# Level clips left out, abs max and scales of two tiles at once, levels and outputs a tile later, in the FFN of a gated cross-attention block

## The reference, cut to what matters

```python
x = x + tanh(g_xattn) * attention(layernorm(x), ctx, ctx, ...)
x = x + tanh(g_ffn) * ffn(layernorm(x), w_gate, w_up, w_down)

def _act_quant(x):
    scale = 127.0 / clip(max(abs(x), axis=-1), 1e-05)
    return clip(round(x * scale), -128.0, 127.0) / scale
def _bitlinear(x, w):          # w is quantized to -1, 0, 1 times a scale
    return einsum('bsi,oi->bso', _act_quant(x), _weight_quant(w))
def ffn(x):
    gate = silu(_bitlinear(x, w_gate))
    up = _bitlinear(x, w_up)
    return _bitlinear(gate * up, w_down)
```

## Time and profile before

| what | us |
|---|---|
| median of 3 runs | 810.11 |
| lowest and highest | 806.78, 812.03 |
| span of the profiled execution, first to last instruction | 806.5 |
| first product of tile 0 (L1015) starts | 700.39 |
| last product, tile 27, starts | 793.34 |

### The profile page before, as it was taken

One profiled execution on the slowest core, in us unless ns is written; L12 is line 12 of the kernel. 1 busy time (PEld: TensorE's weight loads), 2 busy tenths in 40 slices (PEclk: granted clock), 3 DMA queues, 4 the chain that ended last, 5 costly groups with the idle time before them and its releaser, 6 DMA issues.

```text
span 806.5 us, 20948 instructions
## 1 busy us (share of the span) xinstructions
PE 708.8 (88%) x7117; PEld 475.3 (59%) x7127; DVE 720.1 (89%) x1479; ACT 691.7 (86%) x1482; POOL 520.3 (65%) x983
## 2 busy tenths in 40 slices
PE   7568889999999999999999999999998888777886
PEld 5234566666666666666666666666665555433444
DVE  5789899979899898989999999899999868798996
ACT  1578789898999999999999999999898997678884
POOL 4757556667777667676666676767663145376985
PEclk8666699999999999999999999999999999899999
DMA  9997847464667565767545666646563123156567
GB/s 206 202 259 179 176 123 148 106 114 129 153 119 145 123 141 123 147 115 151 127 129 141 126 130 133 128 128 138 114 124 73 45 72 97 52 124 165 137 164 176
DMA packets 148889, 108.50 MB, mean 135 GB/s; under 512 B 56992, under 2 KB 145184, under 8 KB 148768
## 3 DMA queue, kind: packets, MB, share of 16 engines
q1 hardware_dynamic: 143630, 101.98, 57.0%
q10 hardware_dynamic: 5152, 5.19, 2.6%
HBM read 49.54 MB, written 12.85 MB: 77 GB/s over the span
## 4 chain that ended last, share of the span: by engine, by line
PE 45%; DVE 22%; ACT 21%; issue 7%; DMA 2%; POOL 2%; SPq 1%; DVEq 0%; ACTq 0%; POOLq 0%
PE p_o L1327 9%; PE p_m L1405 9%; ACT ex L1179 7%; PE p_s L1310 7%; ACT pt L1169 6%; PE p_t L1348 5%; DVE kst L1015 4%; DVE hmax L1018 4%; PE p_m L1394 4%; DVE stats L890 3%; PE p_m L1386 3%; ACT L1169 2%; ACT L1206 2%; PE p_m L1378 2%; DVE nm L909 2%
## 5 line engine op out<-in xcount | busy, mean ns | idle before, releaser
L1179 ACT ACTIVATE ex<-p_s,nm 112x375 f32<-112x375 f32 x512 | 272.6, 606 | 10.1 <-DVE nm L909 8.9
L1169 ACT ACTIVATE pt<-p_t,ct 128x336 f32<-128x336 f32 x488 | 242.5, 563 | 32.4 <-PE p_t L1348 31.9
L890 DVE BATCH_NORM_STATS2 stats<-ex 112x6 f32<-112x375 f32 x512 | 253.2, 537 | 8.1 <-ACT ex L1179 6.6
L909 DVE TENSOR_REDUCE nm<-p_s 112x2 f32<-112x750 f32 x256 | 236.6, 925 | 2.0 <-PE p_s L1310 2.0
L1310 PE MATMUL p_s<-kst,qst 96*112 96x375 bf16 x512 | 135.8, 350 | 34.3 <-ACT ex L1179 24.8
L1348 PE MATMUL p_t<-qst,kst 99*128 99x112 bf16 x1464 | 115.3, 214 | 3.5 <-ACT pt L1169 2.7
L1348 PEld LDWEIGHTS p_t<-qst,kst 99*128 99x128 bf16 x1464 | 91.3, 98 | 42.9 <-issue 18.7
L1386 PE MATMUL p_m<-wv_sb,ctxt 128*128 128x256 f32 (+1 forms) x384 | 106.3, 400 | 4.0 <-DVE va L842 2.6
L1327 PE MATMUL p_o<-pt,va 128*32 128x112 f32 (+1 forms) x3072 | 102.0, 266 | 1.0 <-ACT ex L1179 0.5
L1405 PE MATMUL p_m<-ctxt,wk_sb 128*128 128x375 f32 x240 | 94.3, 517 | 1.3 <-DVE qf L858 0.7
L1327 PEld LDWEIGHTS p_o<-pt,va 128*32 128x32 f32 (+1 forms) x3072 | 70.8, 111 | 36.9 <-issue 30.7
(11 more groups left out here) (190 smaller groups left out, 1201.3 us busy)
## 6 DMA issues: line engine op xcount, KB each, us to landing
kst<-kp SPq DMA_DIRECT2D x378, 93.8 KB, 3.5
ctxt<-ctxt_dram SPq DMA_DIRECT2D x32, 375.0 KB, 4.2
qbounce<-qp SPq DMA_DIRECT2D x32, 168.0 KB, 2.7
qst<-qbounce SPq DMA_DIRECT2D x32, 168.0 KB, 3.6
qst<-qbounce SPq DMA_DIRECT2D x32, 112.0 KB, 3.4
xm<-x_dram SPq DMA_DIRECT2D x32, 112.0 KB, 2.4
x_dram<-x SPq DMA_DIRECT2D x32, 112.0 KB, 1.9
xt<-x_dram SPq DMA_DIRECT2D x28, 128.0 KB, 2.9
```

Source lines behind the costliest of these rows:

```text
L890: last = nc.vector.bn_stats(stats[:, nb % RING, 2 * pb + i], ex[0:SQ, 2 * (t % 2) + i, :])
L909: nc.vector.tensor_reduce(nm[:, n % RING, 2 * p:2 * p + 2], p_s[t % 2][0:SQ, :, 0:SK], axis=AX.X, op=ALU.max, negate=True).then_inc(s_max, 1)
L1169: nc.scalar.activation(pt[:, (2 * r + i) % 8], st_home(r, i)[:, 0:KC * SQ].rearrange("k (c q) -> k c q", c=KC), ACT.Exp, scale=ct[:, nr % ...
L1179: last = nc.scalar.activation(ex[0:SQ, 2 * ((t - 1) % 2) + i, :], p_s[(t - 1) % 2][0:SQ, i, 0:SK], ACT.Exp, bias=nm[:, ne % RING, h:h + 1])
```

## The change

- The clip of x levels (L712) and of hidden levels (L725, L1039) is left out. POOL and DVE convert the rounded values at once.
- The ring `hh` of products has 4 buffers in place of 2. DVE forms the products of two tiles and then takes the abs max, the scale and the reciprocal of both with one instruction each (`step_of`, `in_step`); the last two tiles, 26 and 27, stay apart.
- The output scale moves from ACT (L1243, each tile) to POOL, one for two tiles.
- ACT rounds tile s - 2 in step s, where it was s - 1. POOL, SP's transposing DMA, the down product and the outputs go a step later with it (`T_LAG` 2 to 3, `Y_LAG` 5 to 6). SP loads the residual rows of tile s - 2.

```diff
-HRING, XRING, T_LAG, Y_LAG, YRING = 4, 8, 2, 5, 4
+HRING, XRING, X_LAG, T_LAG, Y_LAG, YRING = 4, 8, 2, 3, 6, 4
+HHRING = 4
...
+        def step_of(n):
+
+            return n // GROUP if n < TILES - GROUP else n - (TILES - GROUP) // GROUP
+
+        def in_step(j):
+
+            return [n for n in range(TILES) if step_of(n) == j]
...
-                nc.gpsimd.tensor_scalar(fxn[:, i % 2], fxn[:, i % 2], ROUND + 127.0, ROUND - 128.0, ALU.min, ALU.max).then_inc(s_gk, 1)
-                pool.wait_ge(s_gk, count(1, i, 1))
...
             def tile(s):
-                n = s - 1
+                n = s - 2
                 if 0 <= n < TILES:
+                    j = step_of(n)
+                    if n == in_step(j)[0]:
+                        first, end = n, n + len(in_step(j))
+                        pool.wait_ge(s_hsc, count(1, j, 1))
+                        if j == 0:
+                            pool.wait_ge(s_tn, TN_TGD)
+                        nc.gpsimd.tensor_scalar(ysc[:, first:end], hsc[:, first:end], tgd[:, 0:1], 0.0, ALU.mult, ALU.add).then_inc(s_ysc, 1)
...
-                    nc.gpsimd.tensor_scalar(hr[n % HRING][:, half], hr[n % HRING][:, half], ROUND + 127.0, ROUND - 128.0, ALU.min, ALU.max).then_inc(s_hcl, 1)
-                    pool.wait_ge(s_hcl, count(1, n, 1))
...
-                    if n >= 2:
-                        dve.wait_ge(s_hr, count(1, n - 2, 1))
+                    if n >= HHRING:
+                        dve.wait_ge(s_hr, count(1, n - HHRING, 1))
...
-                    nc.vector.tensor_reduce(hmax[:, n:n + 1], hh[n % 2], axis=AX.X, op=ALU.max, apply_absolute_value=True).then_inc(s_hmx, 1)
...
+                    j = step_of(n)
+                    if n == in_step(j)[-1]:
+                        first, end = in_step(j)[0], n + 1
+                        at = first % HHRING
+                        dve.wait_ge(s_h, count(1, n, 1))
+                        nc.vector.tensor_reduce(hmax[:, first:end], hhs[:, at:at + end - first], axis=AX.X, op=ALU.max, apply_absolute_value=True).then_inc(s_hmx, 1)
...
-                n = s - 1
+                n = s - 2
                 if 0 <= n < TILES:
-                    act.wait_ge(s_hinv, count(1, n, 1))
+                    act.wait_ge(s_hinv, count(1, step_of(n), 1))
...
-                    nc.scalar.activation(ysc[:, n:n + 1], hsc[:, n:n + 1], ACT.Copy, scale=tgd[:, 0:1]).then_inc(s_ysc, 1)
```

More of the change, by code:

```diff
@@ L162, in roomy @@
             return [view[:, scale * (first + i * each):scale * (first + (i + 1) * each)] for i in range(ring)]
-        sg, hh, hr = roomy(2, F), roomy(2, F), roomy(HRING, F)
+        sg, hh = roomy(2, F), roomy(HHRING, F)
+        hhs = room[:, 2 * F:(2 + HHRING) * F].rearrange("p (i k) -> p i k", i=HHRING)
+        hr = roomy(HRING, F)
         hq, hqt = roomy(HRING, F, True), roomy(HRING, F, True)
@@ L256, in gated_block @@
         s_gl = [sem(f"s_f_x_group{i}") for i in range(2)]
-        s_ag, s_gx, s_gr, s_gk, s_gq, s_gt, s_gc, s_gs = (sem(f"s_f_x_{i}") for i in ("means", "chain", "rounded", "clipped", "quant", "transposed", "copied", "scales"))
-        s_g, s_u, s_sg, s_h, s_hmx, s_hsc, s_hinv, s_hr, s_hcl, s_hq = (sem(f"s_f_{i}") for i in (
-            "gated", "up", "silu", "h", "hmax", "hscale", "hinverse", "hround", "hclip", "hquant"))
+        s_ag, s_gx, s_gr, s_gq, s_gt, s_gc, s_gs = (sem(f"s_f_x_{i}") for i in ("means", "chain", "rounded", "quant", "transposed", "copied", "scales"))
+        s_g, s_u, s_sg, s_h, s_hmx, s_hsc, s_hinv, s_hr, s_hq = (sem(f"s_f_{i}") for i in (
+            "gated", "up", "silu", "h", "hmax", "hscale", "hinverse", "hround", "hquant"))
         s_ht = [sem(f"s_f_ht{i}") for i in range(HRING)]
@@ L515, in tile @@
                     if n == TILES - 1:
-                        sp.wait_ge(s_hd, 2)
+                        sp.wait_ge(s_hd, 1)
                     if n >= HRING:
@@ L523, in tile @@
                     sp.dma_start(out_rows[P * n:P * (n + 1)], yo[n % YRING]).then_inc(s_out[n % YRING], 16)
-                n = s
+                n = s - X_LAG
                 if 0 <= n < TILES:
@@ L1012, in tile @@
                     dve.wait_ge(s_gs, 4 if n >= EARLY_TILES else 2)
-                    if n >= 2:
-                        dve.wait_ge(s_hr, count(1, n - 2, 1))
-                    nc.vector.scalar_tensor_tensor(out=hh[n % 2].rearrange("p (b k) -> p b k", b=2), in0=p_u[:, :, :], scalar=usc[:, n:n + 1],
+                    if n >= HHRING:
+                        dve.wait_ge(s_hr, count(1, n - HHRING, 1))
+                    nc.vector.scalar_tensor_tensor(out=hh[n % HHRING].rearrange("p (b k) -> p b k", b=2), in0=p_u[:, :, :], scalar=usc[:, n:n + 1],
                                                    in1=sg[n % 2].rearrange("p (b k) -> p b k", b=2), op0=ALU.mult, op1=ALU.mult).then_inc(s_h, 1)
-                    dve.wait_ge(s_h, count(1, n, 1))
-                    nc.vector.tensor_reduce(hmax[:, n:n + 1], hh[n % 2], axis=AX.X, op=ALU.max, apply_absolute_value=True).then_inc(s_hmx, 1)
-                    dve.wait_ge(s_hmx, count(1, n, 1))
-                    nc.vector.tensor_scalar(hsc[:, n:n + 1], hmax[:, n:n + 1], 1e-5, 1.0 / 127.0, ALU.max, ALU.mult).then_inc(s_hsc, 1)
-                    dve.wait_ge(s_hsc, count(1, n, 1))
-                    nc.vector.reciprocal(hinv[:, n:n + 1], hsc[:, n:n + 1]).then_inc(s_hinv, 1)
+                    j = step_of(n)
[4 more added lines that the diff above has]
+                        nc.vector.tensor_reduce(hmax[:, first:end], hhs[:, at:at + end - first], axis=AX.X, op=ALU.max, apply_absolute_value=True).then_inc(s_hmx, 1)
+                        dve.wait_ge(s_hmx, count(1, j, 1))
+                        nc.vector.tensor_scalar(hsc[:, first:end], hmax[:, first:end], 1e-5, 1.0 / 127.0, ALU.max, ALU.mult).then_inc(s_hsc, 1)
+                        dve.wait_ge(s_hsc, count(1, j, 1))
+                        nc.vector.reciprocal(hinv[:, first:end], hsc[:, first:end]).then_inc(s_hinv, 1)
                 if s in LATE_AT:
@@ L1038, in tile @@
                     dve.wait_ge(s_hr, count(1, n, 2))
-                    nc.vector.tensor_scalar(hr[n % HRING][:, half], hr[n % HRING][:, half], ROUND + 127.0, ROUND - 128.0, ALU.min, ALU.max).then_inc(s_hd, 1)
-                    dve.wait_ge(s_hd, 1)
                     dve.wait_ge(s_ht[n % HRING], ring_count(16, n - HRING, HRING))
@@ L1222, in tile @@
                     act.wait_ge(s_y, count(1, n, 1))
-                    act.wait_ge(s_ysc, count(1, n, 1))
+                    act.wait_ge(s_ysc, count(1, step_of(n), 1))
                     if n >= 2:
@@ L1239, in tile @@
                     for half in halves(n):
-                        nc.scalar.activation(hr[n % HRING][:, half], hh[n % 2][:, half], ACT.Copy, scale=hinv[:, n:n + 1], bias=ROUND).then_inc(s_hr, 1)
-                    if n == 0:
-                        act.wait_ge(s_tn, TN_TGD)
-                    nc.scalar.activation(ysc[:, n:n + 1], hsc[:, n:n + 1], ACT.Copy, scale=tgd[:, 0:1]).then_inc(s_ysc, 1)
+                        nc.scalar.activation(hr[n % HRING][:, half], hh[n % HHRING][:, half], ACT.Copy, scale=hinv[:, n:n + 1], bias=ROUND).then_inc(s_hr, 1)
                 if s - 1 in LATE_AT:
```

4 lines of the change are left out of this document (2 added, 2 removed).

## The result

The changed kernel takes 813.25 us (median of 12 runs, 810.22 to 815.38), the kernel before, run beside it, 810.0 us (12 runs, 806.65 to 812.03). The ratio is 1.0040, with a 95% interval from 1.0024 to 1.0056: some 3 us slower, against +1.0 predicted (811.1 us, range 805 to 817). The time lies in the range, and "within 1%" was the likeliest case. But the working has to be looked at term by term, since errors of both signs met in the sum.

A forecast was written before the change was run, and what follows sets the result against it. The prediction took DVE to bound the FFN's steady stretch. Its terms, -0.3 - 0.1 - 0.2 + 2.8 - 1.2 = +1.0 us on the profiled 806.5, gave 807.5; adding 3.6 for the median gave 811.1 us, range 805 to 817.

The forecast's parts named there:

- within 1%: Whole kernel: the case that its time changes by no more than 1% either way; chance 0.81.
- What bounds: Steady stretch of the FFN: DVE is the full engine, 2.93 us a tile, and everything else waits for it.
- The abs max of 2048 elements: DVE's one abs max for a pair: 2.29 us, against two of 1.22 before.
- The middle: Between a pair's two product starts: the second waits for ACT's silu (2.61 us) and PE's refill of `p_u` (2.41 us).
- Tiles 18 to 26: Steady stretch, product 18 to product 26: 26.2 us against 23.4 before, a loss of 2.8 us.
- Rival 2: Pair middles: no wait arises, `p_u` filled and silu ready at 1.31 us; 14 us less, 797 us; chance 0.04.
- Tiles 0 to 10: Product 0 to product 10: five pairs and the table change at tile 9, 35.3 us against 35.39, gain 0.1 us.
- rival 1: Pairs: PE drops to its lower clock, up product 1.86 us, middle 3.23 us; some 8 us more, 819; chance 0.10.
- Tiles 10 to 18: Product 10 to product 18, with late x groups and `rows_scale`: 30.9 us against 31.13, gain 0.2 us.
- pair 14-15: Within tiles 10 to 18: the copies are hidden, so this pair takes 6.4 us.
- The end: After the last products: PE's wait shorter, tile 27's transposed levels some 0.5 us earlier; gain 1.2 us, between 0.3 and 1.8.
- The start: Attention before tile 0: without POOL's x clips stretching DVE's mean subtraction, 0.3 us earlier, between 0 and 1.0.

The follow-up runs named there:

- the two-buffer kernel with the later step: The changed kernel with everything behind the reciprocal one step later and a second PSUM buffer for up products of odd tiles from 19 on: 811.84 us, ratio 1.0015.
- the other ACT order: The changed kernel with ACT, up to step 25, rounding both tiles of a pair in one step, behind the silu of the second tile: 814.83 us, ratio 1.0048.
- the kernel with a lag of three: The changed kernel with rounding, conversion, transposing DMA, down product and output one step later still (tile s - 3 in step s): 816.3 us, ratio 1.0069.
- the one with some pairs: The changed kernel with pairs only at tiles 0-1, 6-7 and 10-11: 805.88 us; with the last four tiles' residual loads two steps earlier too, 805.71 us.

## Why the prediction was right or wrong

**What bounds.** Right. DVE was the full engine, and the price of making it wait outweighed what the batching saved. Two rows were misread on the way, without weight: the up product starts 0.06 us behind the end of the product (774.06, 774.12), not 0.03, and the second scaling of `rows_scale` stood beside POOL's addition, not its conversion.

**The abs max of 2048 elements**: predicted 2.29, measured 2.286 in 13 instances, the ends were 2.14 and 2.44. With 60 ns from the Trainium skill (Perfetto Trace Analysis, Optimizing Scalar/DVE Operations) the prediction estimated 2.38; but that section calls its figures engine-busy times and puts the latency in a profile at about twice as much, and with 0.12 the estimate is 2.32. The line through this operation's own rows, with 0.15, was the better guide. The same section says that breaking instructions up may let work finish sooner where the engine isn't saturated and makes others wait; the rows of tiles 4 and 5 below, where PE waits behind the long abs max, agree.

**The middle**: predicted 2.61 by ACT and 2.41 by PE, measured 2.57 and 2.46 to 2.47. A pair 6.61, measured 6.59. Tiles 18 to 26: 26.2, measured 26.25. Rival 2 (the wait doesn't arise) needed, by its text, `p_u` filled and silu ready; the two-buffer kernel with the later step has both, and wins the middles.

**Tiles 0 to 10** (-0.1, measured +1.25). The step that failed is "3.35 (PE does an output projection ahead of tile 5's products; an estimate)". It took 4.99. (The ends of these pairs with the work outside the middles took 16.74 for 16.75, and the last piece 4.92 for 5.30.) The timeline of DVE and PE there:

```profile
707.97 2.29 DVE L1036 TENSOR_REDUCE hmax<-kst 128x2 f32<-128x2048 f32 x1
...
710.57 0.39 DVE L913 COPY ot<-p_t 128x224 f32<-128x224 f32 x1
...
711.11 1.87 PE L1407 MATMUL p_m<-wo_sb,ot 128*112 128x256 f32 x4 [2.08 <-DVE ot L913]
...
712.77 2.84 PE L1484 MATMUL p_s<-wq,kp 128*128 128x512 bf16 x8
```

The copy for which PE waits now stands behind the long abs max. PE sat idle 2.08 us (1.00 before the change), and from 711 to 715 the granted clock was 0.57 and 0.58, the lower level of 1.2 GHz. In the kernel with two up buffers PE was idle 0.94 us here, the output projection took 1.09 us, seven of the eight gate and up matmuls 1.67, and this middle 3.37; the granted clock was 1.00 from 714 to 718, after 0.57 from 710 to 714. So the estimate holds at the full clock, and rival 1, which I had placed in the steady pairs, came true at a place where I hadn't looked: 4.99 - 3.37 = 1.6 us, in most profiles of kernels with this pair (4.82 to 5.05 in five, 3.37 in two). With tiles 4 and 5 single it is 3.89 or 3.90 in six profiles and 4.83 in one. The one wait doesn't tell which it will be: with the other ACT order PE was idle 1.83 us here and kept the full clock, with all tiles single 1.00 us and lost it. That the long abs max makes the wait is shown; that it makes the clock fall is likely, not shown.

**Tiles 10 to 18** (-0.2, measured +0.32). `rows_scale` behaved as predicted: 0.23 and 0.22 us, product 18 at 5.00 us behind product 17, not 5.4. The step that failed is pair 14-15, "6.4", which took 7.34. Again PE's clock:

```profile
752.27 1.89 PE L1484 MATMUL p_s<-wq,kp 128*128 128x512 bf16 x4 [3.52 <-DVE kst L1029]
```

The x group of step 13 and the end of the pair before held `p_u` and with it PE for 3.52 us. The granted clock from 752 to 754 is 0.56. The middle is 3.32 us; rival 1's sum, 1.31 + 1.86 + 0.06 = 3.23, is its anatomy. In the kernel with the other ACT order, where the granted clock is 1.00 at this place, the same middle is 2.47.

**In the steady pairs** rival 1 didn't come: up matmuls take 1.04 us after waits of 1.12 to 1.25, and the window has the clock at 1.00.

**The end** (-1.2, measured +0.71). PE's wait got shorter, as said (1.65 us for 3.28), and its down products ran at the full clock; a cost was missing. The transposed levels of tile 27 "can be there some 0.5 us earlier than before" is what didn't come: their DMA is issued 6.70 us after product 27, before 5.57. "The lags of a step and the residual loads move SP's DMAs past a later conversion; ... so nothing waits" is the step that failed. It is true of the steady stretch, but at the end one more tile is in flight, and SP issues a transposing DMA, an output and a load more, back to back: 1.24 + 0.58 + 0.43 = 2.25 us. Against the kernel without the hidden clip, whose end also runs at the full clock, the last transposing DMA comes 6.70 - 4.82 = 1.88 us later and the end is 13.87 - 11.45 = 2.42 us longer. The loads' part was taken away by itself (0.94 of the DMA's delay, 0.65 of the end); the rest was not, and the kernel with a lag of three, whose end is 1.3 longer still, points the same way. I had counted PE's and DVE's queues at the end and not SP's.

**The start** (-0.3, measured -2.6). The reason given, POOL's x clips, is not it: without them it is 50.07 us from the first x abs max to product 0, against 50.32. This stage of the kernel before, of the changed one and of the one with some pairs (columns as in the earlier trace rows):

```profile
650.07:700.39 50.32, 41.51 (x578) 29.63 (x576) 36.77 (x114) 40.43 (x86) 24.14 (x43) 0.93 0.29 84
...
649.76:697.75 47.99, 39.77 (x579) 28.96 (x576) 34.23 (x113) 40.46 (x86) 16.48 (x31) 0.96 0.28 84
...
652.50:700.03 47.53, 38.35 (x578) 27.92 (x576) 34.22 (x113) 40.47 (x86) 16.48 (x31) 1.00 0.29 85
```

The granted clock of the stage orders all fourteen profiles: at 1.00 it takes 47.5 us (five kernels), at 0.96 47.8 to 48.0 (three, the changed one among them), at 0.93 48.5 to 50.6 (six: the three without the later steps and three with them). So 2.3 of the 2.6 us go with PE's clock in two single executions, and the part of the change itself isn't told from them. What makes the clock fall there in one execution and not in another stays open.

**The sum.** Terms of +2.76 and -2.64, +1.25, +0.71 and +0.32 give +2.4. The largest term was right and by its mechanism; the others missed by -2.3 and +3.8, which partly cancelled, and the -2.3 goes with the clock of single executions. That the total lay near the forecast is luck to that extent. The medians differ by +3.25, forecast +1.0.

## What to carry to other kernels

Batching on the fullest engine pays only if what feeds it is as deep as the batch: here two up buffers and a rounding that needs no fresh reciprocal. With either missing, a steady pair costs 0.6 to 0.7 us; with both there it wins 0.65. Where two waits of like length stand side by side, taking away one shows next to nothing, and only the kernel without both tells the theory from its rival.

For each step of lag, write out the last three tiles of every queue, the one that issues DMAs included. And for each instruction made longer, ask which small one now stands behind it, and who waits for that.
